# A Mamba-2 and mixture-of-LoRA block on one core: convolution ahead of gating where a tile ends, fixed PSUM banks, and projection halves moved between iterations

## What is computed

```
xn = layernorm(x)
proj = xn @ in_proj_w.T                # gate 8192, hs 8192, B 1024, C 1024, dt 128
hBC = silu(depthwise causal conv of 4 taps(hs, B, C) + conv_b)
dt = clip(softplus(dt + dt_bias), 0, 100);  A = -exp(A_log)
# 128 heads of 64, state 128, 8 groups of B and C, chunks of 128 tokens
Y_diag = (C B^T * L) (hs*dt);  states, Y_off by chunks;  Y = Y_diag + Y_off + hs*D
g = Y * silu(gate);  out = rmsnorm per group of 1024 (g) * norm_w @ out_proj_w.T
x + out + (xn @ base_W.T + top-2-of-8 LoRA experts(xn))
```

## Time and profile before

| | |
|---|---|
| three runs | median 1742.64 us (1741.93 to 1743.99) |
| the profiled execution | 1740.54 us, its span 1739.2 us |
| mean granted TensorE clock | 0.985 |
| TensorE busy | 1640.0 us, 94% |
| VectorE, ScalarE, GpSimd busy | 79%, 71%, 75% |
| chain that ended last | PE 53%, DVE 13%, POOL 13%, ACT 11%, issue 10% |

### The profile page before, as it was taken

One profiled execution on the slowest core, in us unless ns is written; L12 is line 12 of the kernel. 1 busy time (PEld: TensorE's weight loads), 2 busy tenths in 40 slices (PEclk: granted clock), 3 DMA queues, 4 the chain that ended last, 5 costly groups with the idle time before them and its releaser, 6 DMA issues.

```text
span 1739.2 us, 31672 instructions
## 1 busy us (share of the span) xinstructions
PE 1640.0 (94%) x10764; PEld 1316.0 (76%) x10764; DVE 1369.0 (79%) x1669; ACT 1241.8 (71%) x2630; POOL 1295.9 (75%) x1225
## 2 busy tenths in 40 slices
PE   6989999999998999999999999989999899999987
PEld 4767877777787877778777787778778787777766
DVE  5877788877888868887788878887688877888765
ACT  5177777867767777677777777777777777676764
POOL 2047669877788768887688777887688876987776
PEclk9999999999999999999999999999999999999999
DMA  3243356553665446453566545654464535654553
GB/s 126 83 163 102 127 170 176 164 154 110 196 174 166 133 146 201 149 157 116 164 191 181 147 125 176 174 182 119 148 193 149 181 98 166 207 150 140 136 160 105
DMA packets 232527, 265.46 MB, mean 153 GB/s; under 512 B 156072, under 2 KB 157616, under 8 KB 228144
## 3 DMA queue, kind: packets, MB, share of 16 engines
q1 hardware_dynamic: 232368, 263.45, 51.2%
HBM read 162.20 MB, written 69.73 MB: 133 GB/s over the span
## 4 chain that ended last, share of the span: by engine, by line
PE 53%; DVE 13%; POOL 13%; ACT 11%; issue 10%; DMA 0%; SPq 0%; DVEq 0%; ACTq 0%; POOLq 0%
PE P L250 16%; PE P L252 15%; PE P L251 15%; ACT P L539 4%; PE P L436 3%; DVE hsX L729 3%; POOL yb L1089 2%; POOL GL L1013 2%; POOL al L1115 2%; DVE P L978 2%; DVE yb L981 2%; DVE OL L752 2%; DVE Bx L729 2%; ACT P L542 1%; PE P L453 1%
## 5 line engine op out<-in xcount | busy, mean ns | idle before, releaser
L539 ACT ACTIVATE P<-AB,SC 128x128 f32<-128x128 f32 x1024 | 308.3, 365 | 0.5 <-DVE hsX L740 0.5
L250 PE MATMUL P<-xh,AH 128*128 128x512 f32 x656 | 273.3, 417 | 29.1 <-DVE hsX L729 24.2
L252 PE MATMUL P<-xh,AL 128*128 128x512 f32 x656 | 260.8, 398 | 0.0
L251 PE MATMUL P<-xl,AH 128*128 128x512 f32 x656 | 259.9, 396 | 0.0
L729 DVE SCALAR_TENSOR_TENSOR hsX<-P,cwt,hsX 128x1023 f32<-128x1023 f32 x189 | 241.7, 1279 | 15.7 <-ACT hsX L478 11.3
L250 PE MATMUL P<-OH,gTh 128*128 128x512 f32 x512 | 218.1, 426 | 31.2 <-DVE yb L956 29.2
L1089 POOL TENSOR_TENSOR yb<-yb,dhs 128x512 f32<-128x512 f32 x112 | 144.2, 1287 | 136.8 <-DVE yb L956 136.6
L1008 POOL TENSOR_TENSOR AL<-AR,AH 128x512 fp32r<-128x512 f32 x82 | 114.6, 1397 | 169.5 <-ACT AH L465 169.5
L250 PE MATMUL P<-GH,xh 128*128 128x512 f32 x544 | 217.1, 399 | 12.0 <-POOL GL L1013 11.2
L252 PE MATMUL P<-GH,xl 128*128 128x512 f32 x544 | 212.8, 391 | 0.0
L251 PE MATMUL P<-GL,xh 128*128 128x512 f32 x544 | 212.6, 391 | 0.0
(11 more groups left out here) (188 smaller groups left out, 4128.3 us busy)
## 6 DMA issues: line engine op xcount, KB each, us to landing
AB<-acr_d SPq DMA_DIRECT2D x128, 512.0 KB, 5.0
half_d<-hsX SPq DMA_DIRECT2D x60, 512.0 KB, 3.7
AR<-in_wa SPq DMA_DIRECT2D x80, 256.0 KB, 2.8
TS<-in_wg SPq DMA_DIRECT2D x16, 1024.0 KB, 5.2
TS<-in_wo SPq DMA_DIRECT2D x16, 1024.0 KB, 5.6
part_d<-pl SPq DMA_DIRECT2D x64, 256.0 KB, 3.3
pl<-part_d SPq DMA_DIRECT2D x64, 256.0 KB, 2.6
al<-acc_d SPq DMA_DIRECT2D x64, 256.0 KB, 3.0
```

What stands on the lines that cost most here:

```text
L250: te.matmul(o, ah_, bh_, start=(first and i == 0), stop=False)
L251: te.matmul(o, ah_, bl_, start=False, stop=False)
L252: r = te.matmul(o, al_, bh_, start=False, stop=(last and i == n - 1))
L539: r = se.activation(E[:, h, :], AB[m % 2][:, h, :], ACT.Relu, bias=SC[s % 2][:, c, 3, h:h + 1], scale=-1.0)
```

## The change

1. The halves of an even group's tiles become (2, 2, 1, 1, 1, 1, 2, 2). Tiles end at c = 5 and 6 of the even group before and at c = 0, 2, 3 and 4 of the odd group, where before they ended at c = 5, 7, 0, 1, 3 and 4. Those of an odd group stay at c = 6, 0, 2 and 4.
2. Fixed banks: O and BG in 4, Off and GT in 5, St and GTr in 6, Y and T in 7.
3. VectorE: in an iteration in which a tile ends, the convolution stands before the sum and gating, and the decay product after gating. The gate product of the next iteration is at the end, ahead of gTl (and of OL at c = 0). OL 2 and 3 of c = 1 stand behind S.
4. ScalarE: `act_decay` is split; the taps stand between the Relus and Exp, and at c = 7 the second pair of GH does too.
5. POOL: at c = 7, xch comes after the low gate weights.

```
-(2, 1, 1, 2, 2, 1, 1, 2) if s % 2 == 0
+(2, 2, 1, 1, 1, 1, 2, 2) if s % 2 == 0
...
-            jobs += ([in_turn("Off", m)] if c else []) + ([in_turn("St", m)] if c != 7 else []) + [in_turn("Y", m)]
+            jobs += ([("Off", m, (5,))] if c else []) + ([("St", m, (6,))] if c != 7 else []) + [("Y", m, (7,))]
...
+            jobs += [("O", m - 1, (4,))]
+            jobs += [("GT", m + 1, (5,))]
+            jobs += [("GTr", m, (6,))]
...
-                    act_decay(m + 1)
-                    if new_gate:
-                        act_gate_hi(s + 1, (2, 3))
+                    act_relus(m + 1)
                 if m < M:
                     for i in done:
                         act_tap(i)
                 if m + 1 < M:
+                    if new_gate:
+                        act_gate_hi(s + 1, (2, 3))
+                    act_exp(m + 1)
                     act_state_hi(m + 1)
...
+                    if c == 1:
+                        dve_output_lo(s, (2, 3))
+                    if new_tiles:
+                        for i in new_tiles:
+                            dve_conv(i)
+                    elif m + 1 < M:
+                        dve_decay(m + 1)
...
+                    if new_tiles:
+                        if m + 1 < M:
+                            dve_decay(m + 1)
+                    else:
+                        for i in old_tiles:
+                            dve_silu(i)
...
+                if m + 1 < M:
+                    dve_gate(m + 1)
```

More of the change, by code:

```diff
@@ L655, in act_program @@
             act_front(0)
[L656 removed]
+            act_relus(0)
             act_state_hi(0)
+            act_exp(0)
             act_tanh5(1)
@@ L939, in dve_program @@
                 pm, pc, ps = m - 1, (m - 1) % 8, (m - 1) // 8
+                new_tiles = [k // 2 for k in slot_halves[m + 1] if k % 2] if m < M else []
+                old_tiles = [k // 2 for k in slot_halves[m] if k % 2]
                 if m + 1 < M:
                     dve_front(m + 1)
-                if c == 1:
-                    dve_output_lo(s, (2, 3))
-                new_tiles = [k // 2 for k in slot_halves[m + 1] if k % 2] if m < M else []
                 if m < M:
-                    dve_gate(m)
                     if new_tiles:
[L948 to L951, removed]
+                        for i in old_tiles:
+                            dve_silu(i)
                     if c:
@@ L960, in dve_program @@
                             ve.wait_ge(s_sl, n7(m) - 1)
-                        ve.tensor_copy(S[:, :], o).then_inc(s_st, 1)
+                        ve.tensor_copy(S[:, :], bank("St", m)).then_inc(s_st, 1)
                     elif c != 7:
@@ L965, in dve_program @@
                         ve.wait_ge(s_sl, n0(m))
[L966 to L969, removed]
+                        ve.tensor_tensor(S[:, :], bank("St", m), S[:, :], ALU.add).then_inc(s_st, 1)
+                    if c == 1:
[5 more added lines that the diff above has]
+                        dve_decay(m + 1)
                     ve.wait_ge(s_y, m + 1)
@@ L1080, in pool_program @@
                 s, c = divmod(m, 8)
-                if m + 1 < M:
+                new_gate = c == 7 and s + 1 < NS
+                if m + 1 < M and not new_gate:
                     pool_scaled(m + 1)
                 if m < M:
-                    if c == 7 and s + 1 < NS:
+                    if new_gate:
                         pool_gate_lo(2 + s, (0, 1))
@@ L1089, in pool_program @@
                         pe_.tensor_tensor(yb[:, :], yb[:, :], dhs[:, :], ALU.add).then_inc(s_tp, 1)
-                    if c == 7 and s + 1 < NS:
+                    if new_gate:
                         pool_gate_lo(2 + s, (2, 3))
+                        pool_scaled(m + 1)
                     if m + 1 < M:
```

21 lines of the change are left out of this document (8 added, 13 removed).

## The result

The changed kernel takes 1771.37 us (median of 4 runs, 1770.31 to 1772.65) against 1742.94 (4 runs, 1741.93 to 1743.99) for the kernel before: the ratio of times is 1.0163, 95% interval 1.0146 to 1.0181. It is slower by 28.4 us.

The account below looks back on a forecast made before the run. TensorE bounds the kernel, busy 197.23 of 205.40 us a stretch. New pauses 13.15 plus clock 3.5 less 9.5 removed gives +7.15 a stretch, +50 over seven: 1792 us, range 1725 to 1832.

Parts of the forecast that it names:

- What was removed: Pauses for convolution L729 and eviction L956, and the 1.88 us pause: 6.8 idle and 2.7 clock, 9.5 us a stretch.
- GL's wait: Gate projection at c = 7 waiting for the low gate weights L1013: kept at 1.4 us a stretch.
- The ring: Serial ScalarE and VectorE chain through a tile end: 11.4 us against TensorE's 11.64, just fitting at even c = 2, 4, 6.
- c = 7 even: Gating late behind AH, Tanh and two GH pairs: chain 11.8 us against TensorE's 10.65, pause 1.1.
- c = 1 odd: Off waits 1.9 us for the gate product, St 1.35 for gTl, O 0.5 for OL: together 3.75.
- c = 1 even: Off waits 1.6 us for the gate product, St 1.35 for gTl, O 1.0 for OL: together 3.95.
- c = 3, 5 and 6 even: BG waits for pl, written after the square, at even c = 3 and 5: 0.8 us each.
- rival (d): OL 0 and 1 meet POOL's AL subtraction, taking 2.2 instead of 1.4 us: +11 us, inside the forecast's range; no chance given.
- The clock: Slow clock and fresh starts behind the new pauses: 3.5 us a stretch, bounds 0.6 and 8, against 2.7 removed.
- (a): Chain stays below TensorE's time also at c = 7 and 0, no new pauses: -66 us, 1676; chance 0.18.
- (c): Clock falls at every pause: 11.7 us more a stretch, 1824 us; chance 0.10.
- Rival (b): Mainly the queue of c = 1 stays: +0.5 to +3 us a stretch, 1746 to 1765; chance 0.17.

Follow-up runs that it names:

- the kernel of 1702.8 us: Kernel before with the change's halves, OL 2 and 3 behind the evictions, and in odd groups' c = 7 second GH pair before Exp, xch after low gate weights: 1702.79 us.

## Why the prediction was right, and where it was too large

Sign and mechanism held; the forecast said +50 and the medians give +28.

**What was removed** went as put: the waits for the convolution and for L956, and the 1.88 us pause with its slow matmuls. GL's wait, kept at 1.4 us, measures 0.45 in even and 0.27 in odd groups; at odd c = 7 BG's wait for al (0.70) has come beside it.

**The ring.** Even c = 2 is the plain case: ready at 1198.80, the square released by gating at 1210.12, 11.3 us. The prediction had 11.4, against an iteration of 11.64. The table has the pauses of the stretch from m = 71 on beside the terms. Its third column is idle time as the rows list it. The last is what the places cost from start to start: the length of the iterations, transposes to transposes, less TensorE's own time. That time is taken from iterations of the same kind without a pause: 10.62 us (odd) and 10.96 (even) at c = 0, 10.65 at c = 7, 11.32 in the other odd and 11.65 in the other even ones, with 2.72 more for a second half and 0.33 for BG at odd c = 7.

| place | forecast | idle as listed | start to start |
|---|---|---|---|
| c = 7 even | 1.1 | 0.67 (GL 0.45, transposes 0.22) | 1.4 |
| c = 0 odd | 1.6 | 1.00 | 1.4 |
| c = 0 even | 1.15 | 0.45 | 0.65 |
| c = 1 odd | 3.75 | 3.4 (Off 1.41, St 1.98, O 0) | 3.7 (5.3 with the clock's fall) |
| c = 1 even | 3.95 | 3.5 (BG 1.16, St 1.98, O 0.36) | 4.6 |
| c = 3, 5 and 6 even | 1.6 | 0.86 | 1.5 |
| c = 7 odd | 1.4 for all GL | 0.97 (BG 0.70, GL 0.27) | 1.4 |
| sum | 14.55 | 10.85 | 14.7 |

A pause costs more than the idle time beside it. In the rows of odd c = 1 above, the matmuls start 0.23 us apart but are listed with 0.39, so idle time begins to count 0.16 late; and from the first one behind the pause to the next it is 0.34 (1292.84 to 1293.18) instead of 0.23. That is about 0.27 us more for each pause. Even c = 7 shows it over a whole iteration: 12.03 us against 10.65, with 0.67 listed:

```profile
1263.96 0.60 PE L448 MATMUL P<-ident,yb 128*128 128x128 f32 x4
...
1275.99 0.63 PE L448 MATMUL P<-ident,yb 128*128 128x128 f32 x4 [0.20 <-DVE yb L981]
```

**The step that failed is a size, that of what goes away.** The new pauses were made from start to start (a chain less TensorE's iteration), and so measured they are right in sum, 14.7 for 14.55. But the waits of the kernel before were put at their listed idle time, 8.2 us a stretch. From start to start they cost 10.5: its one stretch without a fall of the clock is 202.45 us long, and TensorE's own time in a stretch is 191.9. So 2.3 us a stretch more were won than the sum had.

Place by place the terms are less good than their sum. At even c = 3 and 5 the prediction took gating to end at ready. The rows show otherwise, the transposes and BG on TensorE, then the square on ScalarE:

```profile
1210.44 0.60 PE L448 MATMUL P<-ident,yb 128*128 128x128 f32 x4
1211.47 0.30 PE L312 MATMUL P<-ident,Bx 128*128 128x128 f32 x1 [0.43 <-ACT pl L692]
```

```profile
1210.12 0.63 ACT L687 ACTIVATE sq<-yb 128x512 bf16<-128x512 f32 x1 [3.33 <-DVE yb L981]
```

Gating was over 0.32 us before ready, so BG waits 0.43 for pl (0.6 from start to start) and not 0.8. By the prediction's own sum (11.4 against 11.64) it should have been ahead there; the term was not made from it. At even c = 7 the chain took 11.9 us (ready at 1263.96, square at 1275.88) where 11.8 was put. But GL's two pauses held up TensorE too, so that only 0.22 was left for the transposes; the forecast counted GL's wait apart.

Within c = 1 of even groups the releaser was wrong: I put 1.6 at Off, but BG's wait for al, which stands behind gating in VectorE's queue, comes first (1.16) and covers it. St was put at 1.35 and is 1.98 in both parities; the two OL before it take 2.43 us and not 1.40, which is rival (d), 1.0 where it had 0.8. One reading behind (d) was wrong: at 1265.35 POOL was not at AL, which began at 1268.05, but at its copy of the high half of an older tile (1265.48 to 1266.99). That OL and AL collide is seen only in the changed kernel. The Trainium skill's "SBUF — State Buffer", section "SBUF: two separate sides", has VectorE with two SBUF inputs and GpSimd lock each other out; 1.41 us without POOL's work, 2.43 with AL, 3.14 and 3.36 with two operations of POOL agree with it.

**The clock.** Its sum was right and its parts were not. Length less listed pauses, of the six full stretches, is 196.5 us before and 197.7 after; the one stretch of before in which the clock never fell has 202.44 - 8.26 = 194.2:

```profile
430.60:633.04 202.44, 194.19 (x1310) 156.94 (x1309) 165.57 (x195) 151.55 (x322) 161.92 (x153) 1.00 0.56 161
```

So clock and fresh starts were 2.3 a stretch before (2.7 was put) and are 3.5 after (3.5 was put). But the falls themselves are as many as before. Windows of one microsecond show eleven times 3.4 us at granted clock 0.50 from m = 0 to 119, in either kernel. An iteration with such a fall is 1.5 to 1.6 us longer than the same without one (17.1 against 15.5 at odd c = 0 of the kernel before, 16.6 against 15.1 at its even c = 1). After the change they are one at odd c = 1 in all seven groups, one at even c = 1 in only two, and two at m = 0 and 1. The rest, for which I had 0.6, goes with the starts behind pauses, of which a stretch now has fourteen or fifteen instead of eight, about 0.27 us each. The kernel with tg ahead of OH bears this out: no fall in any stretch, fifteen pauses, and 195.7 us of length less pauses, 1.5 above the 194.2.

The Trainium skill, "TensorE: Matmul & The Clock Gate", "HAM oscillation", would hold none of these pauses for long enough; the rows have 0.50 behind them, so they still disagree. The same page has another section, "A second HAM failure mode: psum-queue depth-cycling", by which short but frequent idle times between groups of matmuls also bring such falls; the prediction passed it over. It allows falls behind pauses as short as these, which the rows have; that their frequency matters no run here shows, since the kernel with tg ahead of OH has fifteen a stretch and no fall.

**Net.** A full stretch was put at +7.15 and is +3.8. In one measure: the waits after the change 14.55 put and 14.7 measured, those before 8.2 put and 10.5 measured, clock and starts +0.8 put where the falls alone gave about -0.3 (2.25 to 1.9). Six full stretches make 20 us too much. The other terms were off too and nearly cancel, which is luck: the first group was put at +0.8 and is +9.4, the seventh stretch at +7.15 and is -1.8, the tail at 0 and is 1.6, together 8 put and 9.2 measured. One half (2.7 us) is projected earlier in the first group and missing from the seventh stretch, which the prediction didn't write down. At m = 0, BG now waits 1.59 us for Gt and the transposes 3.60 for gating, and behind each the clock falls; the kernel before waits about as much from m = 0 to 7 (7.7 us, now 6.6), but without a fall. In the seventh stretch it fell twice before and once after. And some 2.6 us at the start are there before any moved instruction, 92.78 us after the start against 90.17 in code that is the same. They need not be the change's: in the traces of the five experiments whose code up to there is that of the kernel before, the same place comes at 91.5 to 93.6 us. The profiled execution of the kernel before was a quick one, 2.4 us under its median, and that of the change 1.3 over its own; so the spans are 32.1 apart and the medians 28.4.

**What the runs say of the cause.** The prediction gave late gating and OH as one cause. Two runs part them, and either one nearly ends the loss. With tg ahead of OH gating is as late (0.99 us at the transposes of odd c = 0), and 30 us are gone; with gating of c = 0 early and OH still ahead of tg, 24 are gone. Lateness costs because OH, 2.55 us that nobody needs soon, stands between gating and tg. It is not free without OH either: the kernel with tg ahead of OH contains the halves and the two moved OL, which by themselves gave 1710, and takes 31 us more. Of its 8.6 us of idle time a stretch 4.5 are at the transposes and at BG, where the kernel of 1710 has none.

Rivals (a) and (c) fall: no full stretch is near 196 us (the six take 208.2 to 209.1), and there is not a fall at every pause. Rival (b) had nearly the time (1765, 6 us off, where the forecast was 21 off). It had 1 us at c = 7 and 0, 0.5 at BG and 6 at c = 1, the forecast 3.85, 1.6 and 7.7. From start to start they are 3.5, 1.5 and 8.3: the forecast's mechanism, with the wrong size on the other side of the sum. Not tried: fixed banks with a bank of its own for BG, and tg ahead of OH in the kernel of 1702.8 us.

## What to carry to other kernels

Where engines that work in order form a ring, write down for each iteration when the last link ends and when it is needed, and carry the difference on; being late costs most where something long and not urgent stands between the late result and those who wait for it, so let the urgent instruction pass it first (tg past OH: -30 us). Put what goes away and what comes into one sum in one measure, from start to start: a listed pause was 0.27 us short here, and with six or seven pauses more or less that decides a forecast. Run the parts of a change alone and together: the halves with two moved OL gave -32 us, the whole change, which contains both, +28. Before an instruction is moved, read what the other engines do at the moment to which it goes (gTl ahead of OL, which put OL beside two operations of POOL: +20 us).

## What the hardware showed that was not expected

Two OL of VectorE take 1.41 us while POOL is idle, 2.43 beside one AL, 3.14 beside AL and xch, 3.36 beside AL and al. A pause of TensorE costs about 0.27 us more than its listed idle time. And the length of a pause alone doesn't tell whether the clock falls: 1.41 and 1.98 us with three matmuls between them halved it in all seven groups, 1.16 and 1.98 with a projection half and Off between them in two of seven; a single pause of 1.88 us at odd c = 0 did in six of seven groups of the kernel before, and in two of seven where only OL 2 and 3 had been moved.
